# An attention and expert block on one core: the second bias of the expert stage added by VectorE, and three 128-column products in its second layer

## The reference

```python
keys = jnp.einsum('btd,d->bt', x, wr) + br
expert_idx = jnp.mod(jnp.floor(keys).astype(jnp.int32), W1.shape[0])
for e in range(W1.shape[0]):
    h = jax.nn.relu(jnp.einsum('btd,df->btf', x, W1[e]) + b1[e])
    y = jnp.einsum('btf,fd->btd', h, W2[e]) + b2[e]
    out = jnp.where((expert_idx == e)[..., None], y, out)
```

## Time and profile before

| what | value |
|---|---|
| median of 3 runs | 528.84 us (525.24 to 529.77) |
| profiled execution | 523.54 us, its span 521.6 us |
| PE busy | 460.7 us (88%) |
| PEld busy | 322.3 us (62%) |
| DVE busy | 415.5 us (80%) |
| ACT busy | 351.6 us (67%) |
| POOL busy | 371.7 us (71%) |

### The profile page before, as it was taken

One profiled execution on the slowest core, in us unless ns is written; L12 is line 12 of the kernel. 1 busy time (PEld: TensorE's weight loads), 2 busy tenths in 40 slices (PEclk: granted clock), 3 DMA queues, 4 the chain that ended last, 5 costly groups with the idle time before them and its releaser, 6 DMA issues.

```text
span 521.6 us, 15159 instructions
## 1 busy us (share of the span) xinstructions
PE 460.7 (88%) x5014; PEld 322.3 (62%) x5014; DVE 415.5 (80%) x909; ACT 351.6 (67%) x872; POOL 371.7 (71%) x366
## 2 busy tenths in 40 slices
PE   1576277999999999997999999998899999999986
PEld 1245234565665655655999999995556657656644
DVE  5985268977779889786877888886798898998875
ACT  3679125767777777586777777775577667777663
POOL 4428312488888888873777777775988988988971
PEclk9995558899999999999999999999999999999999
DMA  8998522344465578769788888853456545856421
GB/s 233 285 220 306 110 101 74 78 109 106 108 134 130 154 203 247 191 173 274 215 258 247 256 260 268 264 180 96 100 125 134 148 107 138 147 121 136 103 77 57
DMA packets 82970, 87.00 MB, mean 167 GB/s; under 512 B 10624, under 2 KB 66400, under 8 KB 82912
## 3 DMA queue, kind: packets, MB, share of 16 engines
q1 hardware_dynamic: 78816, 77.86, 55.0%
q0 software_dynamic: 4096, 8.40, 6.7%
HBM read 38.87 MB, written 22.04 MB: 117 GB/s over the span
## 4 chain that ended last, share of the span: by engine, by line
PE 43%; issue 15%; POOL 13%; DVE 13%; DMA 6%; ACT 5%; SPq 3%; POOLq 1%; ACTq 0%; DVEq 0%
POOL padd L534 12%; PE psum L1190 9%; PE psum L1225 8%; PE psum L1209 8%; DVE negm L932 4%; PE psum L1267 4%; PE psum L1240 4%; PE psum L1138 3%; DMA stk<-mT 3%; PE psum L1139 3%; PE psum L1140 3%; SPq L318 3%; DVE split L844 2%; DMA acc<-x 2%; DVE padd L808 1%
## 5 line engine op out<-in xcount | busy, mean ns | idle before, releaser
L656 ACT ACTIVATE prob<-psum 128x512 f32<-128x512 f32 x256 | 150.2, 593 | 104.9 <-PE psum L1209 87.5
L932 DVE TENSOR_REDUCE negm<-psum 128x2 f16<-128x512 f32 x256 | 170.7, 683 | 55.1 <-PE psum L1190 49.2
L581 POOL TENSOR_TENSOR padd<-prob 128x512 f32<-128x512 f32 x104 | 126.9, 1220 | 50.9 <-ACT prob L656 47.8
L1209 PE MATMUL psum<-stk 97*128 97x256 f16 x512 | 99.4, 277 | 15.4 <-DMA stk<-mT 11.5
L1190 PE MATMUL psum<-stk 96*128 96x256 f16 x512 | 102.4, 284 | 8.9 <-DVE negm L932 7.2
L534 POOL TENSOR_TENSOR padd<-xTl,padd 128x512 f16<-128x512 f32 x72 | 83.4, 1159 | 34.0 <-DVE padd L1045 34.0
L724 ACT ACTIVATE xTl<-psum,xn_all 128x128 f32<-128x128 f32 x288 | 82.2, 369 | 27.4 <-POOL padd L534 20.4
L550 POOL DMA_INDIRECT xsort<-xn_all,pos x64 | 65.4, 1022 | 14.2 <-issue 13.3
L1190 PEld LDWEIGHTS psum<-stk 96*128 96x128 f16 x512 | 43.4, 100 | 51.4 <-DVE negm L932 21.8
L558 POOL DMA_INDIRECT xn_all<-ysort,pos x64 | 65.6, 1026 | 12.6 <-issue 8.0
L1225 PE MATMUL psum<-prob,vt 128*32 128x256 f32 x1024 | 68.5, 385 | 1.4 <-ACT prob L656 1.4
(11 more groups left out here) (159 smaller groups left out, 888.4 us busy)
## 6 DMA issues: line engine op xcount, KB each, us to landing
stk<-split SPq DMA_DIRECT2D x192, 128.0 KB
xn_all<-wsplit SPq DMA_DIRECT2D x72, 258.0 KB, 4.4
xsort<-oT SPq DMA_DIRECT2D x9, 512.0 KB, 4.3
xTh<-xsort SPq DMA_DIRECT2D x18, 256.0 KB, 4.2
ysort<-xTh SPq DMA_DIRECT2D x18, 256.0 KB, 4.4
out<-acc SPq DMA_DIRECT2D x15, 256.0 KB
acc<-x SPq DMA_DIRECT2D x3, 1024.0 KB, 8.8
xn_all<-W SPq DMA_DIRECT2D x8, 256.0 KB
```

The costliest lines, as they stand in the source:

```text
L581: nc.gpsimd.tensor_tensor(padd[:, bb, hs], prob[:, bb, hs, 0, :], prob[:, bb, hs, 1, :], ALU.add).then_inc(pool_add, 1)
L656: nc.scalar.activation(prob[:, bb, h, :, :].rearrange("p a c -> p (a c)"), bank[st_bank(u, n)], ACT.Exp, scale=SCALE).then_inc(act_exp, 1)
L932: V.tensor_reduce(negm[:, k % 2, col:col + 2], bank[n % 2].rearrange("p (a c) -> p a c", a=2), AX.X, ALU.max, negate=True).then_inc(dve_ma ...
L1209: ins = mm(bank[b][:, kc * T:(kc + 1) * T], stk[0:97, k % 4, 0, h, t0 + kc * P:t0 + (kc + 1) * P], stk[0:97, k % 4, 1, h, t0:t0 + T], star ...
```

## The change

`output` now does twelve matmuls of 128 columns (hh by high, hl by high, hh by low, for each of four blocks), all into the same 128 columns; the bias matmul, sel and b2s are gone, and so is all that built them. `y_out` becomes a scalar_tensor_tensor: 256 times a row of b2t, a table of b2 in float32 that a DMA broadcasts to all partitions, plus the PSUM result. b2t lies in the first half of oT. SP loads it at unit 15, behind the last W2 loads and a wait for pe_wo. The row of b2t depends on the tile's expert, so DVE now reads experts from texp, eight every eighth tile, and does register arithmetic for every tile.

```diff
+        b2t = oT_f[:, 0:E * D]
@@
-                             (b2_f[0:E], b2), (b2_f[32:32 + E], b2),
@@
                     load_w2(E - 2)
                     load_w2(E - 1)
+                    sp.wait_ge(pe_wo, NSB // 2 - 1)
+                    sp.dma_start(b2t, b2.rearrange("e d -> (e d)").partition_broadcast(P)).then_inc(sp_b2, 16)
@@
-            step(nc.gpsimd.memset(sel[:], 0.0))
-            for base in (0, -32):
-                step(nc.gpsimd.affine_select(out=sel[:], in_=sel[:], compare_op=ALU.not_equal, fill=WS,
-                                             base=base, pattern=[[-1, E], [0, P]], channel_multiplier=1))
@@
-                    cast(b2s[0:E, :], b2_f[0:E, :], WS)
-                    cast(b2s[32:32 + E, :], b2_f[32:32 + E, :], WS)
@@
-                low(b2s[32:32 + E, :], b2_f[32:32 + E, :], b2s[32:32 + E, :], WS)
@@
-                V.reduce_sum(ys[:, t % 8, :], bank[2 + t % 2][:, 0:2 * D].rearrange("p (a d) -> p d a", a=2), AX.X
-                             ).then_inc(dve_y, 1)
+                if t == 0:
+                    dve.wait_ge(sp_b2, 16)
+                if t % 8 == 0:
+                    ex.extend(experts_of(t, 8, mybir.EngineType.DVE))
+                V.scalar_tensor_tensor(ys[:, t % 8, :], b2t[:, bass.ds(ex[t] * D, D)], WS * WS, bank[2 + t % 2][:, 0:D],
+                                       ALU.mult, ALU.add).then_inc(dve_y, 1)
@@
-                    hi_lo = w2[:, bass.ds(e * 2 * F + 2 * fc * P, 2 * P)]
                     hi = w2[:, bass.ds(e * 2 * F + 2 * fc * P, P)]
+                    lo = w2[:, bass.ds(e * 2 * F + (2 * fc + 1) * P, P)]
                     f = slice(fc * P, (fc + 1) * P)
-                    if fc < FC - 1:
-                        mm(dst[:, 0:2 * D], hh[:, k, f], hi_lo, start=(fc == 0), stop=False)
+                    mm(dst[:, 0:D], hh[:, k, f], hi, start=(fc == 0), stop=False)
                     mm(dst[:, 0:D], hl[:, k, f], hi, start=False, stop=False)
-                mm(dst[:, 0:D], sel[:, bass.ds(e, 1), :].squeeze(1), b2s[:], start=False, stop=False)
-
-                ins = mm(dst[:, 0:2 * D], hh[:, k, f], hi_lo, start=False, stop=True)
+                    ins = mm(dst[:, 0:D], hh[:, k, f], lo, start=False, stop=(fc == FC - 1))
```

More of the change, by code:

```diff
@@ L89, in attention_moe_block @@
         wr_s = sb("wr_s", [D, 4], F16)
-        sel = sb("sel", [P, E, P], F16)
         b1c = sb("b1c", [P, E * FC], F32)
         route = sb("route", [P, 184], F32)
-        b2s = sb("b2s", [P, D], F16)
         pos = sb("pos", [P, NC], I32)
@@ L110, in attention_moe_block @@
         wr_i, wr_c, wr_d = prob_f[:, 2180:2181].bitcast(I32), prob_f[:, 2181:2182], prob_f[:, 2182:2183]
-        b2_f = prob_f[:, 2432:2432 + D]
         stats = padd_f[:, 0:NC * 6].rearrange("p (c s) -> p c s", s=6)
@@ L163, in attention_moe_block @@
         sp_wf = sem("sp_wf")
+        sp_b2 = sem("sp_b2")
         sp_lw = [sem(f"sp_lw{i}") for i in range(2)]
@@ L272, in _ @@
                              (wo_s[:].rearrange("p g d -> p (g d)"), woT), (b1c[:], b1T),
-                             (b2_f[0:E], b2), (b2_f[32:32 + E], b2),
-                             (wr_f, wr.rearrange("(p o) -> p o", o=1)), (br_f, br.partition_broadcast(P))):
+                              (wr_f, wr.rearrange("(p o) -> p o", o=1)), (br_f, br.partition_broadcast(P))):
                 sp.dma_start(dst, src).then_inc(sp_small, 16)
@@ L506, in router_weights @@
             def router_weights():
-                pool.wait_ge(sp_small, 16 * 10)
+                pool.wait_ge(sp_small, 16 * 8)
                 step(nc.gpsimd.tensor_copy(wr_i, wr_f))
@@ L739, in _ @@
                 if s == 1:
-                    act.wait_ge(sp_small, 16 * 10)
+                    act.wait_ge(sp_small, 16 * 8)
                     act.wait_ge(dve_set, 1)
@@ L790, in _ @@
             V.memset(negm[:], 0.0)
-            V.memset(place, 1.0)
-            V.memset(b2s[:], 0.0).then_inc(dve_set, 1)
+            V.memset(place, 1.0).then_inc(dve_set, 1)
             c = [0]
@@ L857, in weight_lows @@
             def weight_lows():
+                dve.wait_ge(act_cast, 2)
+                low(wq_s[:, 1, :], wq_f, wq_s[:, 0, :], WS)
                 dve.wait_ge(act_cast, 4)
-                low(wq_s[:, 1, :], wq_f, wq_s[:, 0, :], WS)
-                low(b2s[32:32 + E, :], b2_f[32:32 + E, :], b2s[32:32 + E, :], WS)
-                dve.wait_ge(act_cast, 6)
                 low(wk_s[:, 1, :], bank[6][:, 0:256], wk_s[:, 0, :], WS)
@@ L1050, in y_out @@
                     dve.wait_ge(sp_st[t // 4 % 2], t // 8 * 16)
-                V.reduce_sum(ys[:, t % 8, :], bank[2 + t % 2][:, 0:2 * D].rearrange("p (a d) -> p d a", a=2), AX.X
-                             ).then_inc(dve_y, 1)
+                if t == 0:
[4 more added lines that the diff above has]
+                                       ALU.mult, ALU.add).then_inc(dve_y, 1)
+            ex = []
             def finish_unit(u):
@@ L1356, in _ @@
             token_T(2)
-            pe.wait_ge(sp_small, 16 * 10)
+            pe.wait_ge(sp_small, 16 * 8)
             mm(bank[6][:, 0:256], wkvd_f, wkup_f, start=True, stop=True)
@@ L1362, in _ @@
                 if s == 3:
-                    pe.wait_ge(dve_ws, 4)
+                    pe.wait_ge(dve_ws, 3)
                     pe.wait_ge(dve_xTl, 1)
```

## The result

The changed kernel is slower: a median of 555.15 us (553.14 to 559.24, 6 runs) against 527.62 us (525.24 to 529.77, 6 runs) for the kernel before. The ratio is 1.053, interval 1.048 to 1.058; the difference is 27.5 us, where the prediction had 22.0 and 550.8 us. In the profiled executions it is 554.61 against 523.54, 31.1 us.

The account below looks back on a forecast made before the run. It took DVE's cast and GpSimd excluding each other as the bound, with PE's sequencer to become it. Sequencer +13.5, DVE's reads +9 and start and end -0.5 gave +22.0 on 528.84, so 550.8 us, range 537 to 560.

Parts of the forecast that it names:

- The exclusion sets the pitch: Expert stage: DVE's cast cannot get through while GpSimd works, so a tile takes 1.16 + 0.28 + 0.07 = 1.51 us.
- the array's gain is worth nothing: PE's output: twelve matmuls save 0.04 us a tile, 3 us over 72, counted as nothing because the array is not the bound.
- PE's sequencer, +13.5: Register arithmetic from 5 to 8 steps a tile makes PE's sequencer the bound at 1.72 us, 0.19 a tile over 71.
- the slack of 0.17 a tile: PE's sequencer before the change: it needs 1.36 us of the 1.53 us tile, so 0.17 is to spare.
- the need of 1.06: PE's sequencer before the change: its own time a tile without the texp read, taken as 1.06 us from behind long reads.
- DVE's reads, +9: Nine reads of eight registers, 1.67 us each behind the wait for PE, stall the loop 1.0 us each.
- 4.49 less 3.44: Working for one DVE read: PE's hidden(t+3) starts at 4.49 us instead of 3.44, losing 1.0.
- PE's clock falls: Rival, chance 0.02: PE idles about a fifth of each tile and drops to half clock, over 100 us more.
- the 5.3 us that the forecast added: Base time: the profiled execution lay 5.3 us under the median of the runs, so 545.5 became 550.8.
- b2t, 0 with a range to 2.5: New DMA at the expert stage's start: landing between 247.1 and 251.6, first y_out at 249.22; 0 to +2.5 us once, taken as 0.
- y_out does not contend: DVE's y_out has only one SBUF input, so it should take about 0.28 us beside GpSimd; counted as 0.
- the rival of 569: Rival, chance 0.03: y_out waits for GpSimd, pitch 2.1, +0.57 us a tile over 71, 40 us more.

Follow-up runs that it names:

- static_fixed: Changed kernel with PE's W2 slices and the b2t row at fixed places, so no expert reads or register arithmetic for them; 520.90 us, ratio 0.999.
- three_buffers: Kernel before with three buffers for h32 instead of two, so ACT need not wait for GpSimd's tile t - 2; 526.73 us, ratio 0.996.
- order_complete: three_reduce with DVE making both halves of a token tile ahead of the cast, computing everything; 525.83 us, ratio 0.996.
- three_reduce: three_buffers with hid_high's cast done by a maximum over an axis of length one; 530.70 us, ratio 1.005.
- fixed_row: Changed kernel always adding the same b2t row, so DVE has no texp reads or register arithmetic; 538.44 us, ratio 1.032.
- more_arith: Kernel before with hl times W2's low slice in three of four blocks, adding three register computations a tile and no matmul; 539.53 us, ratio 1.036.
- read_ahead: Changed kernel, complete, with DVE reading one expert a tile ahead of its wait for PE, not eight behind it; 543.84 us, ratio 1.031.
- static_reads: Changed kernel with PE's W2 slices at fixed places, so PE has no texp read or arithmetic there; DVE as changed; 543.42 us, ratio 1.043.
- order_static: Changed kernel, W2 slices and b2t row fixed, three h32 buffers, cast by reduce, both token halves ahead of the cast; 519.88 us, ratio 0.984.

## Why the prediction was right

**The exclusion sets the pitch, and the array's gain is worth nothing: right.** static_fixed keeps 1.52 with the cheaper `output`; three_buffers keeps it with another buffer. That the exclusion is what sets it rests on the sum 1.16 + 0.28 + 0.07 and on order_complete, which falls to 1.50 without it. It isn't the only limit there: with it gone and the order kept (three_reduce) another loop is as long or longer. The new order with the plain cast was not tried.

**PE's sequencer, +13.5: the mechanism and the price of a step right, the sum short.** The pitch was forecast as 1.72 and measured as 1.72 to 1.73 in three kernels. Alone the term made the stage 126.8 - 108.6 = 18.2 us longer in fixed_row and 15.9 in more_arith. What was left out are the long reads of texp. The working took a read as 0.30 always. In fixed_row the 72 reads add up to 26.4 us where 72 x 0.302 are 21.7: 4.7 us that the slack of 0.17 a tile mostly hides before the change, and that a sequencer without slack passes on. The excess differs from execution to execution: it is 3.2 in more_arith and 3.1 in the changed kernel itself (24.8 in all). The prediction had even quoted a read of 1.014, as evidence for the need of 1.06, and did not carry it into the new pitch.

**DVE's reads, +9: the mechanism right, the read too short, and one consequence missing.** The signs are there: nine reads behind pe_y, the queue behind each, a stall of the whole loop. The length was taken from SP's row, 1.67; on DVE the nine took 1.85 to 2.53, 20.1 us in all, 2.23 each. The step of the working was 4.49 less 3.44, so 0.56 more would make it 1.6 a read. Measured: from one read's step to the next are eight steps. In the five of these eight cycles at full clock they take 15.1 to 15.9 us, 15.5 in the mean, against 8 x 1.786 = 14.3 in fixed_row: 1.2 a read, 11 for nine. Part of why it is less than 1.6 is that PE's sequencer has worked ahead by the time the read ends: the next two tiles come at 1.52, not 1.72, which gives back 0.4. Against read_ahead, whose mean pitch is 1.753, it is 1.5 a read; how much belongs to PE's long reads and how much to DVE's is known only to some 2 us. Without the sequencer's limit a read costs more, as the prediction said (1.46 against 1.0): in static_reads the stage is 21.6 longer than in static_fixed, 2.4 a read, with two pieces at half the clock and a late b2t (below) among them.

**"PE's clock falls", 0.02: too low, and its price wrong.** It was dismissed because the clock had stayed at 1.00 in windows in which PE was idle a fifth of the time, and it would have been priced for the whole stage. It fell in short pieces instead. PE's idle time here is not spread: around a read the changed kernel has a pause of up to 0.5 for issue, one transpose, and then a wait of 0.9 to 1.5. At 0.50 the starts of neighbouring matmuls are 0.107 apart, not 0.056, 24 of them take 2.6 us, and the three cycles with such a piece take 16.4 to 16.7: 1.0 more than the others each, 3.0 in all.

The sum by what was measured: 13.5 + 4.7 + 11.1 + 3.0 = 32.3, for a stage that grew by 31.7. It takes fixed_row as the base; with read_ahead as the base the first two are 15.9 (124.5 - 108.6) and the last two the remaining 15.8. Either way the mechanism of both terms holds, and their sizes were short. Against the profiled execution of before the forecast was 545.5, and the profiled one after took 554.6: 9.1 short, where the three parts that were too low or missing (4.7 of long reads, 2.1 of DVE's, 3.0 of the clock) add up to 9.8. That the forecast in medians came closer, 550.8 for 555.15, is luck: the profiled execution of before was 4 us under its median and the one after was not, so the 5.3 us that the forecast added for this made up for half of what the terms lacked.

**b2t, 0 with a range to 2.5: right here, by very little.** It was issued at 242.28 and landed 7.0 us later, at 249.3, just when PE ended the first `output`; the read that stands behind both began at 249.43. In static_reads it was issued at 247.98 and took 4.7: DVE sat idle 4.16 us there, about 1.3 of it behind PE's end, so the step with the first read was 5.19. In order_static it makes the only long step of the stage, 3.94. That kernel's first `y_out`:

```profile
251.89 0.29 DVE L1045 SCALAR_TENSOR_TENSOR xTh<-oT,psum 128x128 f32<-128x128 f32 x1 [2.53 <-DMA oT<-b]
```

The range of the prediction was the right one, and the cost is real in some versions of the same program.

**y_out does not contend: right.** All 72 in the changed kernel:

```profile
L1047 DVE SCALAR_TENSOR_TENSOR xTh<-oT,psum x72: 275/289/290, 251.7 to 388.9; 128x128 f32<-128x128 f32 x72
```

275 to 290 ns with GpSimd at work beside it (56 of the 72 lie wholly within one of its instructions) or not. This is the rule of the Trainium skill, page "SBUF — State Buffer", section "Who interferes with whom", by which a DVE instruction with at most one input in SBUF, outside the two-port modes, does not contend with GpSimd; the trace agrees, and the rival of 569 falls.

**Fits within the signs named beforehand:** the transpose's waits put down to issue, a pitch of 1.7 between the reads, `y_out` at 0.28, 0.4 us gained at the start. Against them stand the stage (140.3, not 131), the length of the reads, and the clock, whose fall the prediction had named as a sign of being wrong.

Left open: why the read of eight registers takes DVE 1.85 to 2.53 us and SP 1.67 in the same kernels. PE's reads beside it are not the reason, since static_reads has none and its DVE reads take 1.84 to 2.51. And what decides which reads are followed by half a clock, three in nine here and two in nine there, was not tried. The length of PE's wait alone does not decide it: in the changed kernel the clock fell behind waits of 1.30, 1.39 and 1.42 us and stayed at 1.00 behind one of 1.50. Nor does it need a read by DVE: in read_ahead and order_complete the clock is at 0.50 for 3.4 us from 245, just ahead of the stage as measured here, behind waits of PE for the loaded tokens of 1.90 and 2.84; in three_buffers it stayed at 1.00 behind one of 2.52.

## What to carry to other kernels

Count what a sequencer does in one turn of a loop (each slice chosen by a register, each read of a register) and set it against the pitch, also where the engine itself looks 99% busy: here three steps of 0.12 us cost more than the whole array could have won. Put a register read ahead of the wait that the work behind it needs, and take one register at a time if the gaps are short. And before a saving on one engine is counted, name every loop that holds the same pitch; here the reads and arithmetic, the exclusion and the order on DVE had to go before it was worth 0.05 us a tile.

## What the runs showed of the hardware

- Register reads from SBUF cost by the register and by the engine: one takes 0.302 on PE and 0.305 on DVE, eight take 1.68 on SP and 2.32 on DVE (medians). The Trainium skill, page "DMA: Bandwidth & Descriptors", section "Latency and other measured facts", gives about 600 ns as the floor; no median here is near it, on either side.
- Some reads of one register take up to 1.04 us (PE) or 0.78 (DVE), with no cause that the profile shows. While the sequencer has slack they are mostly hidden, and when it is the bound they add 0.03 to 0.07 us to the mean pitch (1.753 in more_arith and read_ahead, 1.786 in fixed_row, against 1.72).
- In the changed kernel, PE's waits behind DVE's reads (0.9 to 1.5 us in one piece) were followed in 3 cases of 9 by 3.4 us at 0.50 of the clock, in a stage that is otherwise at 1.00; in static_reads (1.6 to 3.2 us) in 2 of 9, behind those of 3.17 and 2.33.
- A maximum over an axis of length one casts 128x512 from float32 to float16 in 0.675 us beside a working GpSimd, where the plain cast takes 0.42 alone, and ended 0.28 behind GpSimd's end or later in all 68 tiles of the kernel before in which it started while GpSimd worked.
